# Layer norm of layers 0 to 2 moved from the end of the layer into the next attention, one sequence at a time

## The reference: what is computed

```
x = _layernorm(x + attn_L(x));  x = _layernorm(x + ffn_L(x))      # L = 0, 1, 2, 3

def _layernorm(x, axis=-1, eps=1e-05):
    m = jnp.mean(x, axis=axis, keepdims=True)
    v = jnp.var(x, axis=axis, keepdims=True)
    return (x - m) / jnp.sqrt(v + eps)
```

## Time and profile before

| what | value |
|---|---|
| median of 3 runs | 3052.54 us (3043.22 to 3072.81) |
| the profiled execution's own time | 3058.93 us |
| its span, from the first to the last instruction | 3056.8 us |
| busy share: PE, DVE, ACT, POOL | 77%, 50%, 48%, 39% |
| mean granted TensorE clock | 0.861 of full speed |

### The profile page before, as it was taken

One profiled execution on the slowest core, in us unless ns is written; L12 is line 12 of the kernel. 1 busy time (PEld: TensorE's weight loads), 2 busy tenths in 40 slices (PEclk: granted clock), 3 DMA queues, 4 the chain that ended last, 5 costly groups with the idle time before them and its releaser, 6 DMA issues. The chain is left out here.

```text
span 3056.8 us, 51859 instructions
## 1 busy us (share of the span) xinstructions
PE 2358.9 (77%) x17870; PEld 1661.4 (54%) x17870; DVE 1527.2 (50%) x4247; ACT 1465.3 (48%) x3592; POOL 1186.3 (39%) x1743
## 2 busy tenths in 40 slices
PE   6999999982917989882399318999796799966861
PEld 4666666652814555542399304555453577745751
DVE  3555555542126999983133325776103466640653
ACT  4666666650525999970022113777223365622321
POOL 2444444443054555423633552332001333307245
PEclk9999999995955999995699655999898699968975
DMA  3000000002213221102111113331000333111222
GB/s 130 1 1 2 1 1 1 2 1 88 66 40 97 69 64 62 56 1 106 50 50 46 44 52 99 91 95 35 7 0 6 103 100 90 47 38 52 84 66 62
DMA packets 100670, 153.37 MB, mean 50 GB/s; under 512 B 17138, under 2 KB 70276, under 8 KB 93380
## 3 DMA queue, kind: packets, MB, share of 16 engines
q1 hardware_dynamic: 88644, 128.33, 13.6%
q0 software_dynamic: 11776, 21.81, 2.4%
HBM read 99.86 MB, written 48.24 MB: 48 GB/s over the span
## 5 line engine op out<-in xcount | busy, mean ns | idle before, releaser
L830 DVE TENSOR_REDUCE A_nmax<-A_S 128x2 f32<-128x512 f32 (+1 forms) x512 | 309.1, 621 | 228.9 <-PE A_S L658 125.1
L172 POOL TENSOR_SCALAR A_prob<-A_prob,A_rinv 128x256 f32<-128x256 f32 x512 | 235.4, 478 | 355.2 <-DVE A_rinv L388 355.2
L782 ACT ACTIVATE A_PT<-A_E 128x512 f32<-128x512 f32 (+1 forms) x512 | 275.9, 546 | 166.1 <-PE A_E L675 91.3
L383 DVE TENSOR_REDUCE A_nmax<-A_S 128x2 f32<-128x512 f32 x256 | 164.8, 685 | 154.9 <-PE A_S L259 154.9
L340 ACT ACTIVATE A_prob<-A_S,A_nmax 128x256 f32<-128x256 f32 x512 | 234.7, 477 | 4.9 <-DVE A_nmax L383 4.9
L1634 POOL DMA_INDIRECT sent<-x_state,L_row x160 | 153.9, 962 | 182.2 <-DVEq L1914 134.3
L1654 POOL DMA_INDIRECT L_rows<-results,L_row x160 | 154.8, 968 | 153.8 <-DMA results<-L_ye 108.1
L1313 DVE TENSOR_SCALAR_CACHE_REDUCE A_D<-A_S 128x256 f32<-128x256 f32 x512 | 193.4, 416 | 18.6 <-PE A_S L1121 18.1
L1134 PE MATMUL A_T<-ident_sb,A_D 128*128 128x128 f32 x1024 | 162.7, 282 | 30.7 <-DVE A_PT L1319 20.6
L1641 POOL COPY L_wr<-L_w 128x1024 f32 (+1 forms) x144 | 104.2, 725 | 202.3 <-PE L_k L1729 124.6
L1319 DVE COPY A_PT<-A_T 128x512 f32<-128x512 f32 x256 | 174.8, 685 | 8.1 <-PE A_T L1134 7.3
(11 more groups left out here) (359 smaller groups left out, 5998.8 us busy)
## 6 DMA issues: line engine op xcount, KB each, us to landing
A_QS<-stack_q SPq DMA_DIRECT2D x144, 192.0 KB
A_KS<-stack_k SPq DMA_DIRECT2D x144, 192.0 KB
L_xe<-sent SPq DMA_DIRECT2D x46, 256.0 KB, 2.9
results<-L_ye SPq DMA_DIRECT2D x46, 256.0 KB, 2.0
stack_q<-A_parts SPq DMA_DIRECT2D x48, 192.0 KB, 2.1
stack_k<-A_parts SPq DMA_DIRECT2D x48, 192.0 KB, 2.3
L_w<-f_w SPq DMA_DIRECT2D x24, 256.0 KB
sent<-A_zeros SPq DMA_DIRECT2D x9, 512.0 KB
```

The lines of the kernel that those rows point to most:

```text
L172: nc.gpsimd.tensor_scalar(prob[:, n % NP, j, t, :], prob[:, n % NP, j, t, :], rinv[:, n % NP, j, t:t + 1], 1.0, ALU.mult, ALU.mult).then_i ...
L383: nc.vector.tensor_reduce(nmax[:, n % NP, j, :], psS[n % 2][j][:], AX.X, ALU.max, negate=True).then_inc(maxed, 1)
L782: nc.scalar.activation(PT[:, n % RING, :], psE[n % 2][:, 0:BLOCKS, :].rearrange("p a b -> p (a b)"), ACT.Exp, scale=scale).then_inc(expd, 1)
L830: nc.vector.tensor_reduce(nmax[:, b % 2, :, h], view, AX.X, ALU.max, negate=True).then_inc(maxed, 1)
```

## The change

Layers 0 and 1 end when their results are stored in DRAM, and layer 2 when `acc` is full. What was the finishing part of the layer is done in the next attention by sequence, ahead of `turn_x` of the sequence. The row numbers and weights are kept in `held`, which outlives the layer, and `last` tells the attention what it has to fetch: K = 1 row a token from layer 0, K = 2 from layer 1, K = 0 (only `acc`) from layer 2. Layer 3 finishes as before. The steps and their slots, relative to the sequence's own first head:

- attention 1 (after layer 0): 2 gathers by GpSimd at -51 and -50; `join_rows` by GpSimd at -42 (two multiplications by the weight, one addition of x); `stats_last` by VectorE at -38; `root_last` and `write_last` by GpSimd at -35; `turn_x` at -30.
- attention 2 (after layer 1): 4 gathers by GpSimd at -54 to -51; `join_rows` by VectorE at -43 (four scalar_tensor_tensor), `stats_last` at -42; `root_last` by GpSimd at -40; `write_last` by VectorE at -38; `turn_x` at -35.
- attention 3 (after layer 2): `join_acc` by GpSimd at -50 (one addition), `stats_last` by VectorE at -45, `root_last` and `write_last` as in attention 2.

`turn_x` and `add_out_bias` wait for `x_ready`. The attentions' streams begin at GET_AT, 19 to 21 slots earlier than before. The core of the diff (the steps of attention 1 that are like those of attention 2 are left out):

```
-def attention_small(nc, name, x_state, consts, w, scratch, scale, causal):
+def attention_small(nc, name, x_state, consts, w, scratch, scale, causal, last):
...
-    FIRST, LAST = X_AT, SLOTS + Y_AT
+    GET_AT, NORM_AT = X_AT - 19, X_AT - 5
+    JOIN_AT, STATS_AT = (X_AT - 8, X_AT - 7) if last["K"] else (X_AT - 15, X_AT - 10)
+    FIRST, LAST = GET_AT, SLOTS + Y_AT
...
                 def add_out_bias(b):
+                    pool.wait_ge(x_ready, TB * (b + 1))
...
+                def get_last(b, i):
+                    tile, k = divmod(i, K)
+                    after(pool, joined_x, JOINED * (b - 1))
+                    pool.indirect_dma_start(lrows[:, b % 2, tile, k, :], None, last["results"],
+                                            bass.IndirectOffsetOnAxis(ap=last["row"][:, k, TB * b + tile:TB * b + tile + 1], axis=0)).then_inc(fetched[b % 2], 16)
+
+                def join_acc(b):
+                    after(pool, l_steps, 4 * (b - 1))
+                    nc.gpsimd.tensor_tensor(ly[:, b % 2], last["acc"][:, TB * b:TB * (b + 1), :], x_state[:, TB * b:TB * (b + 1), :], ALU.add).then_inc(joined_x, 1)
+
+                def root_last(b):
+                    pool.wait_ge(l_steps, 4 * (b + 1))
+                    after(pool, x_ready, TB * (b - 1))
+                    nc.gpsimd.tensor_scalar(lveps[:, b % 2, :], lmv[:, b % 2, :, 1], EPS, None, ALU.add).then_inc(l_rooted, 1)
+                    pool.wait_ge(l_rooted, 2 * b + 1)
+                    nc.gpsimd.tensor_tensor(lrstd[:, b % 2, :], lveps[:, b % 2, :], mhalf[:], ALU.pow).then_inc(l_rooted, 1)
...
                 def turn_x(b):
                     after(pe, v_ready, b)
+                    pe.wait_ge(x_ready, TB * (b + 1))
...
+                def join_rows(b):
+                    dve.wait_ge(fetched[b % 2], 16 * TB * K * (b // 2 + 1))
+                    after(dve, x_ready, TB * (b - 1))
+                    for k in range(K):
+                        after(dve, joined_x, JOINED * b + TB * k if k else 0)
+                        for tile in range(TB):
+                            nc.vector.scalar_tensor_tensor(out=ly[:, b % 2, tile, :], in0=lrows[:, b % 2, tile, k, :],
+                                                           scalar=last["weight"][:, k, TB * b + tile:TB * b + tile + 1],
+                                                           in1=ly[:, b % 2, tile, :] if k else x_state[:, TB * b + tile, :],
+                                                           op0=ALU.mult, op1=ALU.add).then_inc(joined_x, 1)
+
+                def write_last(b):
+                    dve.wait_ge(l_rooted, 2 * b + 2)
+                    for tile in range(TB):
+                        nc.vector.tensor_scalar(x_state[:, TB * b + tile, :], ly[:, b % 2, tile, :], lmv[:, b % 2, tile, 0:1], lrstd[:, b % 2, tile:tile + 1],
+                                                ALU.subtract, ALU.mult).then_inc(x_ready, 1)
...
                 for s in range(FIRST, LAST + 9):
+                    if K and (b := at(s, JOIN_AT)) is not None:
+                        join_rows(b)
+                    if (b := at(s, STATS_AT)) is not None:
+                        stats_last(b)
+                    if (b := at(s, NORM_AT + 2)) is not None:
+                        write_last(b)
                     if (n := head(s)) is not None:
                         row_max(n)
...
-def attention_dist(nc, name, x_state, consts, w, scratch):
+def attention_dist(nc, name, x_state, consts, w, scratch, last):
...
+    GET_AT, JOIN_AT, STATS_AT, NORM_AT = X_AT - 21, X_AT - 12, X_AT - 8, X_AT - 5
...
+                def join_rows(b):
+                    pool.wait_ge(fetched[b % 2], 16 * TB * (b // 2 + 1))
+                    after(pool, l_steps, 4 * (b - 1))
+                    for tile in range(TB):
+                        nc.gpsimd.tensor_scalar(ly[:, b % 2, tile, :], ly[:, b % 2, tile, :], last["weight"][:, 0, TB * b + tile:TB * b + tile + 1],
+                                                None, ALU.mult).then_inc(joined_x, 1)
+                    pool.wait_ge(joined_x, JOINED * b + TB)
+                    nc.gpsimd.tensor_tensor(ly[:, b % 2], ly[:, b % 2], x_state[:, TB * b:TB * (b + 1), :], ALU.add).then_inc(joined_x, 1)
...
-def finish_layer(nc, name, x_state, acc, fetch=None):
...
@@ routed_layer, SP
+                for i in range(2):
+                    sp.wait_ge(stored[i], 16 * len(range(i, NQ, 2)))
@@ routed_layer, GpSimd
+                if not cap2:
+                    return
                 for i in range(2):
                     pool.wait_ge(stored[i], 16 * len(range(i, NQ, 2)))
```

More of the change, by code:

```diff
@@ L1061, in _ @@
+                for s in range(FIRST, LAST + 8):
+                    for i in range(TB):
+                        if (b := at(s, GET_AT + i)) is not None:
+                            get_last(b, i)
+                    if (b := at(s, JOIN_AT)) is not None:
+                        join_rows(b)
+                    if (b := at(s, NORM_AT)) is not None:
+                        root_last(b)
+                        write_last(b)
                     if (b := at(s, QK_AT + 3)) is not None:
@@ L2252, in program @@
             if step == "ffn2":
[L2253 removed]
+                last = signs(layer)
             elif step.startswith("ffn"):
[L2255 removed]
+                routed_layer(nc, layer, x_state, consts, weights(f"f{layer}_"), dram, held)
+                rows = TILES[layer] * P + (1 if layer == 0 else 0)
+                last = {"K": 2, "row": held["row"], "weight": held["weight"], "results": dram["results"][0:rows, :]}
+                if layer == 0:
+                    last.update(K=1, row=held["row"][:, 1:2, :])
             elif layer == 1:
[L2257 removed]
+                attention_dist(nc, f"A{layer}", x_state, consts, weights(f"a{layer}_"), stack, last)
             elif layer >= 2:
[L2259 removed]
+                attention_small(nc, f"A{layer}", x_state, consts, weights(f"a{layer}_"), stack, HD ** -0.5, layer == 3, last)
+                if layer == 3:
+                    later.close()
             else:
```

181 lines of the change are left out of this document (82 added, 99 removed).

## The result

| | kernel before | changed kernel | ratio, 95% interval |
|---|---|---|---|
| first comparison | 3049.57 | 2934.64 (2931.08 to 2945.31) | 0.9616 [0.9559, 0.9672] |
| set 2 of the experiments | 3062.89 | 2945.73 (2939.36 to 2946.56) | 0.9618 [0.9587, 0.9649] |
| set 3 of the experiments | 3105.24 | 3020.00 (3011.72 to 3032.70) | 0.9727 [0.9699, 0.9755] |

The kernel is 115 to 117 us faster where the one before takes 3050 to 3063 us, and 85 us faster where it takes 3105. The forecast was 2928, for the first case. Both conditions came up, on one and the same chip too (sets 2 and 3), and show in code that no run touches: layer 3 takes 356 to 360 us in one and 398 to 404 in the other. What sets them is not known.

The account below looks back on a forecast made before the run. TensorE idles in three stretches between layers and attentions, the first two paced by GpSimd's gathers. 168.2 - 23.8 - 6.8 - 3 - 8 - 2 = 124.6 us off the median 3052.5 gives 2928 us, range 2900 to 2968.

Parts of the forecast that it names:

- What is removed: Stretches between a layer's last stored result and the next attention, after layers 0, 1 and 2: 53.7 + 94.8 + 19.7 = 168.2 us.
- up to 3.3 us go twice: Possible extra gain if the longer wait between blocks belongs to a block with gathers near its end; counted as nothing.
- The waits between blocks stay: Waits behind ScalarE's last write, 4.06 us before attention 1 and 0.77 before attention 3, were to remain.
- The first sequence: Start of attentions 1, 2 and 3: first x later by 9.0, 9.8 and 5.0 us, together 23.8.
- I count no more.: Attention starts: second and third sequences also come later, but the first score waits for stacked q and k anyway; nothing added.
- Attention 1 in full: Full pipeline of attention 1: VectorE pays 0.62 us of statistics for 11 of 16 sequences, 6.8 us, plus 3 for dearer writes.
- The collisions: VectorE's writes of x in attention 1 beside GpSimd's SBUF work: some 30 us dearer to 15 us back; 3 us cost taken.
- Attention 2 in full: Full pipeline of attention 2: VectorE gets 2.3 us more a sequence; 0.6 taken for each of 13 sequences, 8 us.
- The rule that the prediction weighed instead, on descriptors: GpSimd-issued gathers cannot write descriptors while VectorE uses both ports: about 620 ns alone, 3100 beside a copy.
- Rival 2: TensorE stays at the lower clock longer after thinner attention starts: 3 x 7.5 = 22 us, about 2950 us; chance 0.08.
- Signs named beforehand: Trace checks for openings, transposes, periods and gathers; wrong if VectorE waits for `fetched`, writes exceed 1.2 us, GpSimd exceeds 85%.
- Rival 4: Gathers become several times dearer on GpSimd beside VectorE, 170 us lost in attention 2, about 3100 us; chance 0.02.

Follow-up runs that it names:

- set 2 of the experiments: Changed kernel run again unedited, as yardstick for runs on what the moved work costs in attention 2, against the kernel before: 2945.73 us, ratio 0.9618.
- set 3 of the experiments: Changed kernel run a third time unedited, as yardstick for runs trying to mend it, against the kernel before: 3020.00 us, ratio 0.9727.
- the run with both edits: Changed kernel with first gathers ahead of the loads, attention 2's additions spread, and attention 1's GpSimd multiplication written as two: 3015.99 us, ratio 0.9714.

## Why the prediction was right, and where it was not

The total was right (2934.6 for 2928, range 2900 to 2968), in part by luck: attention 2 costs 24.5 us more than forecast, and 16.8 of that come back as 7.6 more removed and as 5.0 and 4.2 less paid in attentions 1 and 3. The mechanism was right where the change is a serial tail against steps in a pipeline; the price of the filling and of the clock was not. In the condition in which the kernel before takes 3105 us the gain is 85 us, a third less than the 124.6 forecast; the prediction knew of no second condition.

1. *What is removed.* 168.2 counted, 58.7 + 97.9 + 19.2 = 175.8 found. The 7.6 more are what the text named and set at nothing, the longer wait between blocks, "up to 3.3 us go twice". "The waits between blocks stay" failed as a statement of place. The wait goes with the gathers: it left the openings of attentions 1 and 2 and came back at their ends, 2.1 us behind attention 1 and 5.3 behind attention 2, 7.4 together. So the 0 that was taken is right as a sum, by luck. That the gathers make it is shown by runs: with attention 1 undone it is 1.0 again behind it, with attention 2 undone or without its gathers 1.7 and 1.8 there, and without the additions alone it stays at 7.0.
2. *The first sequence.* 9.0, 9.8 and 5.0 to the first transpose; 11.2, 10.4 and 5.4 found. The 2.2 of attention 1 are small errors in GpSimd's steps. Two multiplications take 1.21 us where 0.48 was counted, and the two writes 1.58: half of a 128x256 step of another form was the wrong row (the form alone is worth 0.24 us each, by the run with both edits). And the next sequence's gather, which stands ahead of the root, does not lie wholly under the statistics; it holds the root up by 0.5 us.
3. *"I count no more."* This step failed. Not only the first x is late: the transposes of the second and third in attention 2 come at 1693.86 and 1707.77, each chain behind the one before it (VectorE waits 10.14 us for rows), and the pipeline is full 37 us after the first score instead of 30. In attention 1 the DMA queue's step of the earlier trace rows, ten sequences ahead of its last, is 19.9 us later against the opening (1026.96 before, 988.16 after), 8 more than the first score. There too the clock has a part: in the 106 us behind the opening its mean is 0.58, where it was 0.65, which is some 15 us more at the lower level.
4. *Attention 1 in full.* This step had the wrong sign. +0.6 and more a sequence forecast, -0.9 found. The collisions, for which the text gave "up to 15 back" and took 3 to pay, went the other way: writes of x fell from 28.6 to 14.3 us in 300. That is 1.24 a sequence less, the statistics 0.76 more; of the 0.9 about 0.5 is explained so, the rest is not. No run isolates it. Against the opening the last step of the earlier trace rows is 10.0 us later, so about 10 of the 19.9 are won back.
5. *Attention 2 in full.* 0.6 a sequence for 13 sequences, 8 us, was forecast. Found are 0.95 a sequence, but for fewer of them, since the last addition starts 285 us behind the opening; in all 9.1 us between the 129th and the last score matmul. The term came out nearly right, its price for a sequence did not. Four additions were priced at 1.2 us by layer 0, where GpSimd was idle beside them; here they take 1.66 + 0.61:

```profile
1858.36 1.15 POOL L591 TENSOR_TENSOR A_parts<-A_rest,A_parts 128x512 bf16<-128x512 f32 x1
1858.75 1.66 DVE L907 SCALAR_TENSOR_TENSOR A_ly<-A_lrows,weight,x_state 128x128 f32<-128x128 f32 x2
1859.48 0.78 POOL L609 TENSOR_TENSOR A_xb<-x_state,A_bo 128x256 f32<-128x256 f32 x1
...
1860.44 0.61 DVE L907 SCALAR_TENSOR_TENSOR A_ly<-A_lrows,weight,A_ly 128x128 f32<-128x128 f32 x2
```

   The first two lie beside GpSimd's additions, the next two beside small steps, and at 1678.83 with GpSimd idle the first two take 0.61 as well. The Trainium skill (SBUF — State Buffer, section "Who interferes with whom") says that a VectorE instruction with two inputs in SBUF contends with a GpSimd instruction that reads SBUF. By that rule the pair is dear here and cheap there; the trace agrees, 1.66 against 0.61. The rule that the prediction weighed instead, on descriptors, did not show: gathers had a median of 947 ns in attention 2 and 1080 in attention 1.
6. *Rival 2, the clock,* had 0.08 and is the largest single miss. In attention 2 the clock rises 132 us behind the opening and not 88, and between the first score and the 129th score matmul 14.8 us are lost. Without the gathers the rise comes 60 us earlier and this stretch is 24.1 us shorter, which is the 0.4 a us again; so most of the loss is put down to the clock here, but no run holds the filling as it is and moves the clock alone. The forecast's 17.8 for attention 2 had 9.8 for the start and 8 for the full part. Found are 12.9 to the first score, 14.8 in the filling, 9.1 in the full part and 5.3 behind the block. In attention 3, where no row is gathered, the clock rises 63 us behind the opening, 64 before.
7. *Signs named beforehand.* Two signs of error came true: VectorE waited for fetched rows in attention 2 (24.1 us, five times, 23.6 of them up to 1720), and the first score came 11.9 and 13.0 us later, where 11 was the bound. Two did not: writes of x in attention 1 at 0.72 us on average, GpSimd busy 231 of 300 us. Of the signs of being right, the opening 4 us after the last result did not come (1.2), nor the longer period of attention 1 (24.8 for 26.3 to 26.6).
8. *Rival 4* was excluded rightly: gathers stayed at 0.95 to 1.13 us.

Open: what sets the moment at which the clock rises. Gathers in attention 2 move it from 67 to 127 us, TensorE's own idle time in the first 40 us does not (66 transposes changed nothing), and with attention 2 undone it rose 115 us behind the opening in one condition, 88 in the other. Open too are what sets the length of the wait behind a block with gathers, and whether the falls in the full part come from the short waits of TensorE for A_nmax (longest 1.3 us there, 0.4 where the clock holds) or make them.

## What to carry to other kernels

Work that is moved from a serial tail into a pipeline is paid twice: per step where it shares the bound engine, and once at the filling, where every early sequence waits for the chain of the moved steps and not only the first; price the filling by sequence. Gathers issued in a block lengthen the wait behind it, so moving them moves that wait with them. Price a VectorE step from a row in which GpSimd does beside it what it will do beside it in the new place, and a GpSimd step from a row of the very same form. And where the granted clock is below full for part of a stage, a change of that stage's start moves the rise too, here by 44 us, so that the sum needs a term for it.

## What the runs showed of the hardware

- A GpSimd tensor_scalar over 128x128 with a scalar for each row took 602 ns with one operation, 366 with two multiplications (one of them by 1.0), and 798 with subtract and multiply by two scalars for each row.
- Sixty-six transposes lifted the granted clock of a nearly idle stretch for moments only, to a mean of 0.59 in 20 us; in the full stretch behind it TensorE stood at 0.50 for some 50 us, with 40.00 us busy in a window of 40.
- With the same code, attention 2 kept a clock of 1.00 in one condition and fell to a mean of 0.87 in the other, with 1264 and 1042 matmuls in 150 us.
- Sixty-four gathers issued by GpSimd in attention 2 lengthened the time from its last write to the next block's first transpose from 1.8 to 7.0 us, thirty-two in attention 1 that from the last write to the next block's opening from 1.0 to 3.1.
